# Convolution stages of layers 1 and 2: stores and residual loads on ScalarE's queue, image loads that wait for the products alone

## The chip, the cores and the metric

One core of a Trainium2 chip. The metric is the device time of one execution in microseconds (us).

## What is computed

An input x of 16 images of 32 channels of 128 x 128 float32 passes through four layers, each x = x + L(groupnorm(x)). Cut to what matters:

```python
# layer 1 begins with a convolution of the normalised image (18 offset channels, of which 9 are used)
offset = conv2d(gn(x), offset_conv_w, offset_conv_b, padding=[(1, 1), (1, 1)])   # 3 x 3
...
# layer 2 is one convolution, 32 to 32 channels, and the residual
x = x + (conv_general_dilated(gn(x), weight, (1, 1), ((1, 1), (1, 1))) + bias)   # 3 x 3
```

Layers 0 and 3 and the rest of layer 1 (a state-space model, a deformable gather) are untouched by the change.

## The kernel before, in words

The program runs one stage after the other, with a barrier of all engines between them. `conv_layer` (L508) is built twice: as stage `l1o` (layer 1, no residual, 16 channels stored, into `offsets`) and as stage `l2` (layer 2, with residual, 32 output channels, into the next x). Both handle B = 16 images, one after the other, with two buffers (u = 0, 1).

- **Load** (L536, SyncE): an image lands in `img` three times, shifted by one row up, none and one down, in partitions 0 to 31, 32 to 63 and 64 to 95 (dy = 0, 1, 2). Each copy is one DMA of 2032 or 2048 KB (L540), followed by a small one with the norm's scale and bias into `gn` (L542). With a residual, four DMAs of 512 KB follow (L546), which bring the same image again into `res`, a quarter of its rows in each quarter of the partitions.
- **Normalise** (L568, ScalarE): waits for the six DMAs of the image (`img_in`), and applies scale and bias in place in 11 activations (L575), then counts up `norm_done`.
- **Products** (L582, TensorE): for each of NS = 8 banks, 12 matmuls of 96 x 512 (L596), then `conv_done` goes up by one. The first bank of an image waits for `evac_done` of the image before.
- **Eviction** (L600, VectorE): waits for `stored[u]` and `res_in[u]`, then one instruction for each bank (L622 without a residual, L619 with one) adds bias (and residual) into `ot`, and `evac_done` goes up by one.
- **Store** (L549, SyncE): waits for the eight evictions of the image, then issues four DMAs (L553), of 256 KB each in `l1o` and of 512 KB in `l2`.

What orders the work around the change is SyncE's program: load(0), load(1), and then for each image i: store(i), with its wait, and behind it load(i + 2) into the buffer just used. An image load therefore stands behind the wait for the evictions, and behind the issue and the transfers of the store, in one queue. ScalarE issues no DMA in these stages.

Of the kernel before, what the change touches and what calls it, by code (L numbers as in the profile page):

```python
# [5 lines left out]
ACT = mybir.ActivationFunctionType  # L6
# [4 lines left out]
H = 128  # L11
W = 128
# [25 lines left out]
def at(first, n=1):  # L38

    return bass.ds(first, n)  # L40
# [467 lines left out]
def conv_layer(nc, stage, x, table, weights, bias, out, B, residual):  # L508
    C, WP = T, W + 2
    keep = out.shape[1]  # L510
    QR = H // 4
    RR = 512 // W
    NS = QR // RR
    with ExitStack() as ctx:
        m = Memory(nc, ctx, stage)
        img = m.sb("img", [P, 2, H, WP])
        gn = m.sb("gn", [3 * C, 2, 2])
# [11 lines left out]
        @block.sync  # L529
        def _(sp):  # L530
            sp.dma_start(wt[:, :, :], weights).then_inc(w_in, 16)
            for g in range(4):
                sp.dma_start(bc[C * g:C * (g + 1), :], bias.rearrange("(p a) -> p a", a=1)).then_inc(w_in, 16)
            sp.wait_ge(zeroed, 2)

            def load(b, u):  # L536
                for dy in range(3):
                    lo, hi = max(0, 1 - dy), min(H, H + 1 - dy)
                    part = slice(C * dy, C * (dy + 1))
                    sp.dma_start(img[part, u, lo:hi, 1:W + 1],  # L540
                                 x[at(b), :, lo + dy - 1:hi + dy - 1, :].rearrange("b c h w -> (b c) h w")).then_inc(img_in[u], 16)
                    sp.dma_start(gn[part, u, :], table.rearrange("b (c q) s -> b c q s", c=C)[at(b), :, 0, :].rearrange("b c s -> (b c) s")).then_inc(img_in[u], 16)  # L542

                if residual:
                    for q in range(4):
                        sp.dma_start(res[C * q:C * (q + 1), u, :],  # L546
                                     x[at(b), :, QR * q:QR * (q + 1), :].rearrange("b c h w -> (b c) (h w)")).then_inc(res_in[u], 16)

            def store(b, u):  # L549

                sp.wait_ge(evac_done, b * NS + 2 * NS)
                for q in range(4):
                    sp.dma_start(out[at(b), :, QR * q:QR * (q + 1), :].rearrange("b c h w -> (b c) (h w)"),  # L553
                                 ot[C * q:C * q + keep, u, :]).then_inc(stored[u], 16)

            load(0, 0)
            load(1, 1)
            with sp.Fori(0, B // 2 - 1) as j:
                for u in range(2):
                    store(j * 2 + u, u)  # L560
                    load(j * 2 + u + 2, u)
            for u in range(2):
                store(B - 2 + u, u)
            for u in range(2):
                sp.wait_ge(stored[u], (B // 2 + 1) * 64)

        @block.scalar
        def _(act):  # L568
            with act.Fori(0, B // 2) as j:
                for u in range(2):  # L570
                    act.wait_ge(img_in[u], j * 96 + 96)

                    def norm(part, rows):
                        v = img[part, u, rows, 1:W + 1]
                        return act.activation(v, v, ACT.Identity, scale=gn[part, u, 0:1], bias=gn[part, u, 1:2])  # L575

                    norm(slice(C, 2 * C), slice(0, 1))
                    norm(slice(2 * C, 3 * C), slice(0, 1))
                    norm(slice(0, 2 * C), slice(H - 1, H))
                    for k in range(NS):  # L580
                        ins = norm(slice(0, 3 * C), slice(max(1, k * H // NS), min(H - 1, (k + 1) * H // NS)))
                    ins.then_inc(norm_done, 1)  # L582

        @block.tensor
        def _(pe):
# [2016 lines left out]
```

## Time and profile before

| what | us |
|---|---|
| median of 3 runs | 24395.71 (24389.47 to 24419.06) |
| profiled execution, its own time | 24396.36 |
| its span in the trace | 24394.8 |
| stage `l1o`, from the barrier to the next stage | about 797 |
| stage `l2`, from the barrier to the next stage | about 883 |

The span is one execution as the hardware profiler records it, and the profiled execution's own time is 1.6 us above it. PE is TensorE, PEld its weight loads, DVE is VectorE, ACT is ScalarE, POOL is GpSimd; SPq and ACTq are DMA issues of SyncE and of ScalarE. Times of rows count from the start of the span. The share of the DMA engines can pass 1, since packets of one engine overlap.

### The profile page before, as it was taken

How to read it: one execution, taken by the hardware profiler on the slowest of the kernel's cores; microseconds unless marked ns; L12 is line 12 of the kernel's file. 1: busy time of each engine (PE TensorE's matmuls, PEld its weight loads, DVE VectorE, ACT ScalarE, POOL GpSimd, SP SyncE). 2: the span in 40 equal slices, each digit the busy share in tenths (PEclk: the TensorE clock that was granted, in tenths of full speed). 3: DMA queues.
4: the chain of work that ended last, by engine and by line, in shares of the span. 5: the costliest groups of instructions: out<-in, count | busy, mean ns of one | idle time of the engine just before them, and what ended most of it. 6: DMA issues, size and time to landing. Idle time of an engine off the chain costs nothing. (4 is left out here: it accounts for less than half of the span.)

```text
span 24394.8 us, 385684 instructions
## 1 busy us (share of the span) xinstructions
PE 19768.2 (81%) x135184; PEld 8014.9 (33%) x135184; DVE 15076.5 (62%) x15737; ACT 13799.3 (57%) x22826; POOL 8849.7 (36%) x5553
## 2 busy tenths in 40 slices
PE   6888888886438888888868999994468888888999
PEld 2333333332112222222215555551123333333444
DVE  8999999998138888888855666564143333333011
ACT  6889999896336666666636877783322222222111
POOL 6777778785017777777750000000000000000000
PEclk9999999998769999999988998797789999999999
DMA  1000000001950000000022111126920000111011
GB/s 65 11 12 12 11 12 12 12 11 64 158 116 18 18 18 18 18 17 18 18 69 35 34 34 37 30 38 151 198 71 23 23 23 23 29 24 30 31 43 43
DMA packets 1301498, 995.53 MB, mean 41 GB/s; under 512 B 748392, under 2 KB 1157584, under 8 KB 1265112
## 3 DMA queue, kind: packets, MB, share of 16 engines
q1 hardware_dynamic: 1199560, 849.64, 16.3%
q0 software_dynamic: 26624, 100.67, 1.5%
q10 hardware_dynamic: 74448, 33.14, 0.5%
q8 instruction: 608, 9.96, 0.2%
q14 instruction: 258, 2.11, 0.0%
HBM read 771.60 MB, written 211.63 MB: 40 GB/s over the span
## 5 line engine op out<-in xcount | busy, mean ns | idle before, releaser
L270 DVE TENSOR_TENSOR l_mx<-l_p_v,l_puN 128x2048 f32<-128x2048 f32 x2560 | 5636.5, 2282 | 151.6 <-PE l_p_s L485 138.7
L485 PE MATMUL l_p_s<-l_mx,l_w2z 128*32 128x512 f32 x32768 | 3827.9, 611 | 579.8 <-ACT l_mx L397 315.3
L290 POOL TENSOR_TENSOR l_mx<-l_pv,l_puP 128x2048 f32<-128x2048 f32 x1024 | 3715.6, 3644 | 321.8 <-PE l_p_s L485 316.0
L2103 PE MATMUL l3a_p<-l3a_xn,l3a_w 128*128 128x512 f32 (+1 forms) x6144 | 2680.9, 599 | 271.1 <-ACT l3a_xn L1994 271.1
L1157 DVE TENSOR_TENSOR_SCAN l1m_hs<-l1m_da,l1m_carry,l1m_pu 128x512 f32<-128x512 f32 x2304 | 2824.4, 1268 | 105.9 <-ACT l1m_da L1073 2.2
L2209 POOL DMA_DIRECT2D l3b_xt<-x_after x64 | 33.9, 529 | 7644.3 <-DVE l3b_most L2338 5818.0
L1206 POOL TENSOR_TENSOR l1m_hc<-l1m_hs,l1m_cs 128x1024 f32<-128x1024 f32 x1152 | 2708.7, 2351 | 9.2 <-DVE l1m_hs L1157 5.7
L1815 ACT ACTIVATE l1d_ab<-l1d_pt 128x1024 f32<-128x1024 f32 x2304 | 2299.4, 1024 | 706.9 <-PE l1d_pt L1569 693.0
L416 ACT ACTIVATE l_mx<-l_pv,l_puP 128x128 f32<-128x128 f32 x8192 | 2446.8, 393 | 0.8
L1693 DVE TENSOR_SCALAR l1d_hat<-l1d_ab 128x1024 f32<-128x1024 f32 x2304 | 1623.0, 704 | 818.9 <-ACT l1d_ab L1815 516.4
L397 ACT ACTIVATE l_mx<-l_mx 128x2048 f32<-128x2048 f32 x1024 | 1954.4, 1909 | 49.5 <-POOL l_mx L290 48.9
L485 PEld LDWEIGHTS l_p_s<-l_mx,l_w2z 128*32 128x32 f32 x32768 | 984.6, 112 | 3020.9 <-issue 1760.6
L1147 DVE TENSOR_TENSOR l1m_pu<-l1m_pu,l1m_bs 128x512 f32<-128x512 f32 x2304 | 1477.5, 687 | 749.3 <-PE l1m_pu L902 749.0
L1073 ACT ACTIVATE l1m_da<-l1m_pr,l1m_an 128x512 f32<-128x512 f32 x2304 | 1457.2, 683 | 823.4 <-PE l1m_pr L895 772.8
L902 PE MATMUL l1m_pu<-l1m_dts,l1m_sl 32*128 32x512 f32 x4608 | 1420.7, 692 | 534.8 <-ACT l1m_da L1073 525.9
L2231 PE MATMUL l3b_ps<-l3b_in,l3b_wc 128*128 (+2 forms) x3888 | 1638.2, 583 | 127.7 <-DMA l3b_in<-pooled 102.9
L2103 PEld LDWEIGHTS l3a_p<-l3a_xn,l3a_w 128*128 128x128 f32 (+1 forms) x6144 | 1094.1, 178 | 1857.9 <-issue 1857.9
L1604 PE MATMUL l1d_po<-l1d_hat,l1d_ring 128*32 128x128 f32 x36864 | 1640.6, 300 | 49.8 <-DVE l1d_hat L1693 45.8
L2118 PE MATMUL l3a_pc<-l3a_r,l3a_c 128*32 128x512 f32 x12288 | 1357.7, 605 | 270.7 <-issue 270.7
L1877 POOL TENSOR_TENSOR l1d_res<-l1d_res,l1d_xr 128x512 f32<-128x512 f32 x128 | 168.7, 1319 | 3540.6 <-ACT l1d_res L1824 3540.6
L895 PE MATMUL l1m_pr<-l1m_dts,l1m_sl 32*128 32x512 f32 x4608 | 1407.8, 689 | 2.7 <-ACT l1m_da L1073 2.7
L2005 ACT ACTIVATE l3a_r<-l3a_p 128x512 f32<-128x512 f32 x512 | 306.3, 598 | 1810.2 <-PE l3a_p L2103 1810.2
(301 smaller groups left out, 26624.6 us busy)
## 6 DMA issues: line engine op xcount, KB each, us to landing
n_xt<-x_after SPq DMA_DIRECT2D x48, 2048.0 KB
l3a_xb<-x_after SPq DMA_DIRECT2D x352, 256.0 KB, 4.1
l1o_img<-x_after SPq DMA_DIRECT2D x32, 2032.0 KB, 17.3
l_img<-x_after SPq DMA_DIRECT2D x32, 2032.0 KB, 16.9
l1m_sq<-seq SPq DMA_DIRECT2D x256, 144.0 KB
n_xt<-in_x_dram SPq DMA_DIRECT2D x16, 2048.0 KB
l_xs<-in_x_dram SPq DMA_DIRECT2D x128, 256.0 KB, 2.9
x_after<-l_ot SPq DMA_DIRECT2D x128, 256.0 KB, 2.4
```

Of the source, the lines that this page charges most:

```text
L270: v.tensor_tensor(mx[:, r % QB, :, :, :], columns.unsqueeze(1).broadcast_to([P, 4, G, P]), rows.broadcast_to([P, 4, G, P]), ALU.max).then_ ...
L290: g.tensor_tensor(mx[:, r % QB, :, :, :], pv[:, u, :, :].unsqueeze(1).broadcast_to([P, 4, G, P]), rows.broadcast_to([P, 4, G, P]), ALU.add ...
L397: act.activation(tile, tile, ACT.Relu).then_inc(max_by_g, 1)
L416: ins = act.activation(mx[:, r % QB, q, t, :], pv[:, u, t, :], ACT.Relu, bias=puP[:, u, t, R * q + r:R * q + r + 1])
L485: ins = pe.matmul(p_s[R * q:R * (q + 1), 512 * u:512 * (u + 1)], w2z[:, 31 - r:63 - r], mx[:, r % QB, q, :, :].rearrange("p t v -> p (t v) ...
L1157: dve.tensor_tensor_scan(hs[:, p % 3, part, :], da[:, p % 3, part, :], pu[:, LC * bank:LC * (bank + 1)], carry[:, u, c:c + 1], ALU.mult, A ...
L1206: g.tensor_tensor(hc[:, (3 * u + p) % 6], hs[:, p % 3], cs[:, u:u + 1, :].broadcast_to([NB, 2, LC]), ALU.mult).then_inc(hc_done, 2)
L1604: ins = pe.matmul(po[C * g:C * (g + 1), 512 * (s % 2):512 * (s % 2) + P], ring[:, (8 * u + s + k) % RING, g, k, :], hat[:, m % 3, n % 2, P ...
L1693: v.tensor_scalar(hat[:, m % 3], ab[:, m % 2], 1.0, 1.0, ALU.min, ALU.subtract).then_inc(hat_done, 1)
L1815: act.activation(ab[:, m % 2].rearrange("p a n -> p (a n)"), pt[:, 1024 * (m % 2):1024 * (m % 2 + 1)], ACT.Abs).then_inc(abs_done, 1)
L2103: ins = pe.matmul(acc[0:n, 512 * (ch % 2):512 * (ch % 2 + 1)], w[:, dx, :], xn[:, k % 2, r:r + RC, dx:dx + W], start=dx == 0, stop=dx == 2)
L2231: ins = pe.matmul(bank(name, u, rows * size), wc[:, k, tap, :], src[:, at((i + u) * rows + tap // 3, rows), tap % 3:tap % 3 + size], start ...
```

## The change

Stores and residual loads move from SyncE's program to ScalarE's, with four (`l1o`) or eight (`l2`) DMA issues for each image. ScalarE's order becomes: the residual loads of images 0 and 1, normalise(0), and then for each image i: normalise(i + 1), store(i) with its wait for the evictions, residual load(i + 2). SyncE keeps the image loads alone, and load(i + 2) waits for the 8 banks of image i in `conv_done` instead of `evac_done`. Sizes, matmuls, activations and evictions stay as they are.

```diff
--- before.py
+++ after.py
@@ -541,45 +541,56 @@
                                  x[at(b), :, lo + dy - 1:hi + dy - 1, :].rearrange("b c h w -> (b c) h w")).then_inc(img_in[u], 16)
                     sp.dma_start(gn[part, u, :], table.rearrange("b (c q) s -> b c q s", c=C)[at(b), :, 0, :].rearrange("b c s -> (b c) s")).then_inc(img_in[u], 16)
 
-                if residual:
-                    for q in range(4):
-                        sp.dma_start(res[C * q:C * (q + 1), u, :],
-                                     x[at(b), :, QR * q:QR * (q + 1), :].rearrange("b c h w -> (b c) (h w)")).then_inc(res_in[u], 16)
-
-            def store(b, u):
-
-                sp.wait_ge(evac_done, b * NS + 2 * NS)
-                for q in range(4):
-                    sp.dma_start(out[at(b), :, QR * q:QR * (q + 1), :].rearrange("b c h w -> (b c) (h w)"),
-                                 ot[C * q:C * q + keep, u, :]).then_inc(stored[u], 16)
-
             load(0, 0)
             load(1, 1)
             with sp.Fori(0, B // 2 - 1) as j:
                 for u in range(2):
+                    sp.wait_ge(conv_done, (j * 2 + u) * NS + NS)
+                    load(j * 2 + u + 2, u)
+
+        @block.scalar
+        def _(act):
+            def normalise(u, loads):
+                act.wait_ge(img_in[u], loads * 96)
+
+                def norm(part, rows):
+                    v = img[part, u, rows, 1:W + 1]
+                    return act.activation(v, v, ACT.Identity, scale=gn[part, u, 0:1], bias=gn[part, u, 1:2])
+
+                norm(slice(C, 2 * C), slice(0, 1))
+                norm(slice(2 * C, 3 * C), slice(0, 1))
+                norm(slice(0, 2 * C), slice(H - 1, H))
+                for k in range(NS):
+                    ins = norm(slice(0, 3 * C), slice(max(1, k * H // NS), min(H - 1, (k + 1) * H // NS)))
+                ins.then_inc(norm_done, 1)
+
+            def load_residual(b, u):
+                for q in range(4):
+                    act.dma_start(res[C * q:C * (q + 1), u, :],
+                                  x[at(b), :, QR * q:QR * (q + 1), :].rearrange("b c h w -> (b c) (h w)")).then_inc(res_in[u], 16)
+
+            def store(b, u):
+                act.wait_ge(evac_done, b * NS + 2 * NS)
+                for q in range(4):
+                    act.dma_start(out[at(b), :, QR * q:QR * (q + 1), :].rearrange("b c h w -> (b c) (h w)"),
+                                  ot[C * q:C * q + keep, u, :]).then_inc(stored[u], 16)
+
+            act.wait_ge(zeroed, 2)
+            if residual:
+                load_residual(0, 0)
+                load_residual(1, 1)
+            normalise(0, 1)
+            with act.Fori(0, B // 2 - 1) as j:
+                for u in range(2):
+                    normalise(1 - u, j + (1 + u))
                     store(j * 2 + u, u)
-                    load(j * 2 + u + 2, u)
+                    if residual:
+                        load_residual(j * 2 + u + 2, u)
+            normalise(1, B // 2)
             for u in range(2):
                 store(B - 2 + u, u)
             for u in range(2):
-                sp.wait_ge(stored[u], (B // 2 + 1) * 64)
-
-        @block.scalar
-        def _(act):
-            with act.Fori(0, B // 2) as j:
-                for u in range(2):
-                    act.wait_ge(img_in[u], j * 96 + 96)
-
-                    def norm(part, rows):
-                        v = img[part, u, rows, 1:W + 1]
-                        return act.activation(v, v, ACT.Identity, scale=gn[part, u, 0:1], bias=gn[part, u, 1:2])
-
-                    norm(slice(C, 2 * C), slice(0, 1))
-                    norm(slice(2 * C, 3 * C), slice(0, 1))
-                    norm(slice(0, 2 * C), slice(H - 1, H))
-                    for k in range(NS):
-                        ins = norm(slice(0, 3 * C), slice(max(1, k * H // NS), min(H - 1, (k + 1) * H // NS)))
-                    ins.then_inc(norm_done, 1)
+                act.wait_ge(stored[u], (B // 2 + 1) * 64)
 
         @block.tensor
         def _(pe):
```

## Rows read from the trace of the kernel before

**Rows 1.** Both stages (windows): busy us of five engines, TensorE clock, DMA share, GB/s
```profile
6079.00:6876.00 797.00, 365.65 (x3072) 97.88 (x3072) 124.12 (x135) 274.23 (x176) 0.00 (x0) 0.73 0.98 147
16790.00:17673.00 883.00, 364.46 (x3072) 97.58 (x3072) 124.10 (x135) 274.25 (x176) 0.00 (x0) 0.71 1.03 190
```

**Rows 2.** Who waited for whom, layer 1's stage, then layer 2's
```profile
ACT l1o_img L575 <- DMA l1o_gn<-norm_table: 498.8, 16, 82.9
...
SPq L553 <- DVE l1o_ot L622: 74.8, 12, 38.6
...
SPq L553 <- DVE l_ot L619: 45.1, 2, 44.7
```

**Rows 3.** Timeline of layer 1's stage, one image: start us, us, engine and line
```profile
6328.38 17.17 ACT L575 ACTIVATE l1o_img<-l1o_img,l1o_gn 32x128 f32<-32x128 f32 x11 [28.77 <-DMA l1o_gn<-norm_table]
...
6355.47 11.47 SPq L542 DMA_DIRECT2D l1o_gn<-norm_table  x1
...
6368.61 0.75 DVE L622 TENSOR_SCALAR l1o_ot<-l1o_acc,l1o_bc 128x512 f32<-128x512 f32 x1 [1.82 <-PE l1o_acc L596]
6369.53 5.18 SPq L553 DMA_DIRECT2D offsets<-l1o_ot  x4
...
6374.90 1.99 SPq L540 DMA_DIRECT2D l1o_img<-x_after  x1
```

**Rows 4.** Timeline of layer 2's stage, SyncE's queue, one image
```profile
17054.31 1.87 SPq L546 DMA_DIRECT2D l_res<-x_after  x4
17056.47 1.85 SPq L553 DMA_DIRECT2D x_after<-l_ot  x4
```

**Rows 5.** Timeline: first load of layer 2's stage, and ScalarE's normalisations
```profile
16824.83 0.32 SPq L540 DMA_DIRECT2D l_img<-x_after  x1
...
16863.67 17.16 ACT L575 ACTIVATE l_img<-l_img,l_gn 32x128 f32<-32x128 f32 x11 [83.02 <-DMA l_gn<-norm_table]
16910.05 17.17 ACT L575 ACTIVATE l_img<-l_img,l_gn 32x128 f32<-32x128 f32 x11 [29.21 <-DMA l_gn<-norm_table]
16961.64 17.17 ACT L575 ACTIVATE l_img<-l_img,l_gn 32x128 f32<-32x128 f32 x11 [34.42 <-DMA l_gn<-norm_table]
...
17619.73 17.17 ACT L575 ACTIVATE l_img<-l_img,l_gn 32x128 f32<-32x128 f32 x11 [33.49 <-DMA l_gn<-norm_table]
...
6238.52 17.17 ACT L575 ACTIVATE l1o_img<-l1o_img,l1o_gn 32x128 f32<-32x128 f32 x11 [36.76 <-DMA l1o_gn<-norm_table]
...
6822.33 17.17 ACT L575 ACTIVATE l1o_img<-l1o_img,l1o_gn 32x128 f32<-32x128 f32 x11 [26.08 <-DMA l1o_gn<-norm_table]
```

**Rows 6.** Transfer rate within single phases of an image (windows; last column GB/s)
```profile
16957.00:16966.00 9.00, 0.00 (x0) 0.00 (x0) 0.00 (x0) 4.33 (x5) 0.00 (x0) 0.50 1.09 221
16967.00:16970.00 3.00, 0.00 (x0) 0.00 (x0) 0.00 (x0) 3.00 (x3) 0.00 (x0) 0.50 0.93 360
16974.00:16981.00 7.00, 2.06 (x12) 0.61 (x16) 0.00 (x0) 4.80 (x3) 0.00 (x0) 0.50 1.25 174
16986.00:16993.00 7.00, 7.00 (x68) 1.93 (x64) 2.25 (x3) 0.00 (x0) 0.00 (x0) 1.00 1.02 177
6281.00:6287.00 6.00, 0.00 (x0) 0.00 (x0) 0.00 (x0) 4.53 (x5) 0.00 (x0) 0.55 1.21 142
```

**Rows 7.** DMA packets of an image's first copy, then of its second
```profile
DMA packets 2375, 1.21 MB, mean 174 GB/s; under 512 B 2, under 2 KB 2375, under 8 KB 2375
...
DMA packets 128, 1.05 MB, mean 175 GB/s; under 512 B 0, under 2 KB 0, under 8 KB 0
```

**Rows 8.** Two queues at once, in 12625 to 12630 us: packets, MB, share
```profile
q1 hardware_dynamic: 418, 0.83, 67.7%
q10 hardware_dynamic: 411, 0.11, 12.3%
```

**Rows 9.** Timeline at 12620 us: DMA issues of ScalarE and of SyncE
```profile
12620.08 11.97 ACTq L1325 DMA_DIRECT2D rows<-l1y_piece  x1
...
12630.03 0.30 SPq L1275 DMA_DIRECT2D l1y_f<-seq  x1
```

## The prediction

> **What bounds the kernel now.** First the busy times of the two stages: in 797 and 883 us the fullest compute engine, TensorE, works 366 us, while the DMA share is 0.98 and 1.03 [rows 1]. So the transfers are full and no engine is. The table of waits says the same: in `l1o` ScalarE's idle time, 498.8 us, all ends with the image's DMAs [rows 2]. What the change can touch is how SyncE keeps the queue filled. In `l2` its wait for the evictions cost 45.1 us in only 2 waits, 44.7 of them the last one, after all loads: over the 14 images between it never waits, so the queue never runs out. In `l1o` there are 12 waits, 74.8 us; without the last (38.6 us) that is 36.2 us in 11, some 3.3 us each [rows 2]. In the timeline the reader sees how close it is: the eviction ends at 6369.36, four store issues take 5.18 us, and only at 6374.90 the next image load goes out [rows 3].
>
> Then the sizes. An image is 2.10 MB; it is copied three times (6.26 MB, two copies lack a row), the residual is 2.10 MB, the store 2.10 MB in `l2` and 1.05 MB in `l1o`. Rates by phase [rows 6]: image copies 174 to 177 GB/s, residual 221, store of `l2` 360, store of `l1o` 142. That makes 35.8 us for the copies, 9.5 for the residual, 5.8 and 7.4 us for the stores. Sum for `l2`: 51.1 us an image; ScalarE's normalisations start 13 x 50.6 us apart from the third to the last (16961.64 to 17619.73) [rows 5]. **`l2` is its transfers, one after the other.** Sum for `l1o`: 43.2 us; measured 44.9 (6238.52 to 6822.33 over 13) [rows 5]. The 1.7 us are the queue running dry around the waits.
>
> A second bound is the turn of one buffer, which carries every second image. From the start of a normalisation to the end of the last eviction: 6328.38 to 6369.36, 41.0 us [rows 3]; from the issue of a load on an empty queue to its normalisation: 16824.83 to 16863.67, 38.8 us [rows 5].
>
> **The change, part by part.**
>
> *The wait and the issue ahead of the image load.* The load waits for `conv_done`, one eviction (0.75 us) earlier than before, and the 5.2 us of store issue are gone from SyncE (in `l2` 1.87 + 1.85 us for eight issues [rows 4]). Behind SyncE's new wait stand image loads alone. In `l1o` a buffer's turn becomes 40.2 + 38.8 us plus the store's 7.4 us of transfer, which still falls into every load: 86.4, or 43.2 us an image, by chance the same as the sum of the transfers (40.2 is 41.0 less the 0.75). So of the 1.7 us at most all goes. Two bounds that meet seldom both hold without a gap, and the store now stands at another place of the load, so I take half, 0.8 us: 13 x 0.8 = 10 us less. Ends: 0 and 22 us less. In `l2` a turn is (40.2 + 38.8 + 15.3)/2 = 47.2 us an image, under 50.6; the transfers bound it, and the earlier release is worth nothing, because what covers it is the image load still under way.
>
> *Eight (four) issues on ScalarE.* ScalarE works 17.2 us for an image [rows 5] and has 33.4 us to spare in `l2`, 27.7 in `l1o`. At SyncE's price the issues cost it 3.7 and 5.2 us, beside the transfers: nothing. Store(i) now goes out behind normalise(i + 1), when evictions of i have long ended (41.0 us after normalise(i) began, with the next normalisation ending at 50.6 + 17.2), so its wait is free; its store is needed, and the residual too, only at the first eviction of i + 2, some 50 us later. Nothing is late there.
>
> *Two queues on the same DMA engines.* No stage of the change has shown this, so I bound it by the one place where both queues are full, at 12625 us: SyncE's queue 418 packets of 2 KB, ScalarE's 411 of 256 bytes [rows 8]. The engines take one packet from each in turn, whatever its size. An image's first and third copies are packets of 512 bytes (1.21 MB in 2375), its second of 8 KB (1.05 MB in 128) [rows 7]; stores and residuals I take to be as large or larger. So when ScalarE's burst comes, the image stream all but stands, for the 15.3 us (7.4 in `l1o`) that the burst would have taken in line anyway: **the sum stays**. Only against the second copy's packets would there be real sharing, and the burst begins 17.2 us and a few us of latency after an image has landed, when the second copy (11.9 to 23.9 us) is nearly through. I take a gain of 0.5 us an image in `l2`, 13 x 0.5 = 6.5 us less; ends: 2 us of gain (26 us less) to 0.5 us of loss from disturbing (6.5 more). The Trainium skill, "DMA: Bandwidth & Descriptors", section "Queues, rings and completion order", says that an engine drains a whole packet, typically 9 to 17 descriptors, from one queue before it turns to the next. If the 512-byte pieces went in such groups, the image stream would go on during the burst, which is the second rival's case; the equal counts above speak for single pieces.
>
> *Residual loads at the start and end of `l2`.* Before, residual 0 followed image 0, residual 1 image 1, and residual 15 came last, hidden under the last normalisation. Now residuals 0 and 1 go out with image 0: normalise(0) comes 2 x 9.5 = 19 us later, at 16882.7, image 1 lands 9.5 us later than its 16910.05, at 16919.6, and the products of image 0 end at 16882.7 + 40.2 = 16922.9, with the queue dry for some 5 us. Image 2 is normalised at 16922.9 + 38.8 + 15.3 = 16977, against 16961.64: **15 us more**, never won back, since transfers bound the rest. Ends: 10 (the residual's own time alone) and 20. `l1o` has no residual.
>
> Sum: -10 - 6.5 + 15 = -1.5 us, on the profiled execution's 24396.36 us (span 24394.8): 24395. The runs' median, 24395.71, is the same to 0.7 us. With the ends: from -22 - 26 + 10 = -38 to 0 + 6.5 + 20 = +27, 24358 to 24423.
>
> **The rivals.**
>
> *Faster: the burst is hidden in the image stream.* For it: image copies move only 175 GB/s, stores 360 [rows 6], so an engine that waits on a small copy could move a store meanwhile. Against it: the one-for-one turn. If half of each burst were hidden, `l2` would take max(35.8 + 7.65, (79.0 + 7.65)/2) = 43.5 us an image: 13 x 7.1 less, 15 more, 77 us less; `l1o` max(39.5, 41.4) = 41.4: 13 x 3.5 = 46 less. Together 24273.
>
> *Slower: ScalarE's issues wait behind SyncE's.* The small DMA behind an image copy sits in issue for 11.47 us [rows 3], while that copy's packets are made. If making them held up ScalarE's issues too, its normalisations would start late, in `l2`, where it issues eight. It decides from 33.4/8 = 4.2 us an issue. At one long wait for every two issues, 4 x 11.5 + 17.2 = 63.2 us an image: 13 x 12.6 = 164, and 15: 24575 (in `l1o`, 2 x 11.5 + 5.2 + 17.2 = 45.4, no change worth counting). Against it: ScalarE's issue of 11.97 us from 12620.08 was under way when SyncE issued at 12630.03 in 0.30 us [rows 9]. The Trainium skill, "Perfetto Trace Analysis", section "DMA Instruction — HWDGE (DVE, Sync)", has descriptor generation as one block, locked for one sequencer at a time; by that rule this rival would hold, and the row says that it is no lock for the length of an issue.
>
> **How the numbers follow.** About 0.2% (49 us) is what a measurement of this kernel can tell from no change. My forecast gets 0.78: its ends lie within 0.2%, but terms that I have not seen may carry 0.03 of it below and 0.01 above. Hidden bursts get 0.16, of which 0.01 would stay within 0.2%; held-up issues 0.06. So faster 0.03 + 0.15 = 0.18, same 0.74 + 0.01 = 0.75, slower 0.01 + 0.06 = 0.07. The range takes my ends, widened below to 24335 for bursts hidden in a small part, above to 24428; about 2 in 10 lie outside, in the rivals' full prices.
>
> **What would show it.** In the changed kernel: normalisations of `l2` 50 us apart from the third on, those of `l1o` 44; the first of `l2` some 58 us after the first load's issue instead of 38.8; SyncE's image loads waiting for TensorE, not for VectorE; ScalarE's issues of 0.3 to 1.3 us each. `l1o` some 787 us, `l2` some 892. I am wrong if the interval in `l2` is under 48 us (bursts hidden), or if ScalarE shows issues of several us (held up), or if the DMA rate during a burst is well above the two phases' own.

## The result, and the profile after

| what | before | after |
|---|---|---|
| median of 12 runs each, side by side | 24401.65 (24341.51 to 24473.11) | 24321.45 (24244.69 to 24380.95) |
| ratio to before, with its 95% interval | 1 | 0.9962 (0.9948 to 0.9976) |
| profiled execution, its own time | 24396.36 | 24289.5 |
| its span | 24394.8 | 24287.9 |

The changed kernel is 80 us faster by the medians, and by the interval 59 to 127 us faster. The forecast was 24395, with 24335 to 24428 around it: it said no change, and the time came out below the range.

Where did it go? First the two stages, in windows from stage start to stage end (columns as in [rows 1]).

```profile
6074.00:6799.00 725.00, 367.82 (x3072) 98.71 (x3072) 123.98 (x133) 274.25 (x176) 0.00 (x0) 0.74 0.96 161
16686.00:17565.00 879.00, 366.98 (x3072) 98.79 (x3072) 123.58 (x133) 274.24 (x176) 0.00 (x0) 0.71 1.02 190
```

TensorE, VectorE and ScalarE do what they did before, in 725 us instead of 797 in `l1o`, in 879 instead of 883 in `l2`. The rate in `l1o` rose from 147 to 161 GB/s [rows 1]. Measured in the same way for every kernel below, from the first instruction of one stage to that of the next:

| stage | before | after | difference |
|---|---|---|---|
| `l1o` | 799.6 | 730.0 | -69.6 |
| `l2` | 882.7 | 884.0 | +1.3 |
| deformable gather, untouched | 3827.5 | 3783.9 | -43.6 |
| all others | 18885.0 | 18890.0 | +5 |

The two stages of the change give -68 us, which lies inside the interval. The 43.6 us of the gather are its own scatter: over the profiled executions of this case it took 3764 to 3910 us with the same instructions. So the experiments are read by the lengths of the two stages, which repeat within 2 us in `l1o` (730.0, 731.3 and 731.3 in the changed kernel, e8 and e9, whose `l1o` loops are the same). In `l2` they repeat less well: in four kernels whose `l2` loop is the same (the changed kernel, e9, e10 and e11) the distance between two normalisations was 49.5, 48.8, 47.9 and 49.5 us, a spread of 1.6 us an image or 21 us a stage.

The normalisations (start us, us, engine, line) give the distance: in `l1o` from the third to the last 13 x 40.2 us, where it was 44.9 [rows 5]. In `l2` the first comes 58.0 us after the first load's issue (first row of the second fence), the third 152.4, and from there it is 13 x 49.5 to the last, where it was 50.6 [rows 5].

```profile
6225.68 0.99 ACT L558 ACTIVATE l1o_img<-l1o_img,l1o_gn 32x128 f32<-32x128 f32 x2 [28.87 <-DMA l1o_gn<-norm_table]
6748.57 1.00 ACT L558 ACTIVATE l1o_img<-l1o_img,l1o_gn 32x128 f32<-32x128 f32 x2 [23.34 <-DMA l1o_gn<-norm_table]
```

```profile
16716.88 0.33 SPq L540 DMA_DIRECT2D l_img<-x_after  x1
...
16774.85 0.99 ACT L558 ACTIVATE l_img<-l_img,l_gn 32x128 f32<-32x128 f32 x2 [102.70 <-DMA l_gn<-norm_table]
...
16869.24 0.99 ACT L558 ACTIVATE l_img<-l_img,l_gn 32x128 f32<-32x128 f32 x2 [42.03 <-DMA l_gn<-norm_table]
...
17513.20 0.99 ACT L558 ACTIVATE l_img<-l_img,l_gn 32x128 f32<-32x128 f32 x2 [31.45 <-DMA l_gn<-norm_table]
```

Now the waits of SyncE in the changed `l1o` (engine and line waiting, what it waited for: total us, times, longest), and of ScalarE in the same stage:

```profile
SPq L540 <- PE l1o_acc L607: 84.4, 14, 10.6
ACT l1o_img L558 <- DMA l1o_gn<-norm_table: 429.5, 16, 82.4
```

The image load waits for TensorE, 14 times, 6 us each. Before, SyncE waited in front of the stores, 3.3 us in 11 waits [rows 2]. A wait that is longer in a stage that is shorter means that SyncE had sent off the last image load early: in `l1o` the queue is no longer what is short, the turn of one buffer is. In `l2` there is one such wait, for image 2 at the start, where the prediction had the queue run dry for some 5 us; over the rest the transfers bound it still:

```profile
SPq L540 <- PE l_acc L607: 11.6, 1, 11.6
```

The timeline around one store of `l1o` shows where the store went (start us, us, engine, line):

```profile
6385.11 8.40 SPq L542 DMA_DIRECT2D l1o_gn<-norm_table  x1
6386.29 1.50 ACT L558 ACTIVATE l1o_img<-l1o_img,l1o_gn 32x128 f32<-32x128 f32 x3 [25.24 <-DMA l1o_gn<-norm_table]
6387.55 0.32 ACTq L575 DMA_DIRECT2D offsets<-l1o_ot  x1
6387.70 1.97 ACT L558 ACTIVATE l1o_img<-l1o_img,l1o_gn 96x1920 f32<-96x1920 f32 x1
6388.03 1.27 ACTq L575 DMA_DIRECT2D offsets<-l1o_ot  x3
```

ScalarE issues the four DMAs in 1.8 us here (5.18 us on SyncE before [rows 3]; in 6 of the loop's 14 images they took ScalarE 4.9 to 5.1 us as well), and not behind its normalisation but 1.3 us after that has begun, while its activations run. What the engines then move, in windows of GB/s (last column) of the image copy before the store's packets, of a store with few image packets beside it, and of a store beside image packets:

```profile
6388.00:6393.00 5.00, 0.00 (x0) 0.00 (x0) 0.00 (x0) 5.00 (x3) 0.00 (x0) 0.50 1.26 174
6394.00:6398.00 4.00, 0.00 (x0) 0.00 (x0) 0.00 (x0) 4.00 (x3) 0.00 (x0) 0.50 1.14 319
6353.00:6360.00 7.00, 0.00 (x0) 0.00 (x0) 0.00 (x0) 7.00 (x5) 0.00 (x0) 0.50 1.12 284
```

The image copy runs at its old 174 GB/s [rows 6]; store and copy together come to 319 and 284. The store's own 1.05 MB in the second window passed in 3.6 us, 290 GB/s, where before it took 9.6 us (109 GB/s) from its first packet to its last. The packets of that third window by queue (q1 is SyncE's, q10 ScalarE's: packets, MB, share):

```profile
q1 hardware_dynamic: 1896, 0.97, 68.7%
q10 hardware_dynamic: 124, 1.02, 43.0%
```

In 7 us nearly the whole store (1.02 of 1.05 MB) and 0.97 MB of image came through; the image alone would have moved 1.22 MB at 174 GB/s. The store cost the image 1.4 us here, not 7.4, and the queues did not take turns one for one. Of ScalarE's 124 packets 62 are the store's, of 16 KB; the other 62 have 4 bytes. So 62 packets of the store stand against some 1890 of the image.

In `l2` a burst is a store and a residual load. Its window, 17 us from 17024, shows less of this: 0.86 MB of image beside 3.93 MB, where the image alone would have moved 2.96 MB.

```profile
q10 hardware_dynamic: 347, 3.93, 80.7%
q1 hardware_dynamic: 1058, 0.86, 29.0%
```

The two halves of the burst differ. The first two lines are 7 us of the store (17024 to 17031), the next two 9 us of the residual load (17032 to 17041):

```profile
q10 hardware_dynamic: 165, 1.88, 67.4%
q1 hardware_dynamic: 878, 0.55, 46.1%
...
q10 hardware_dynamic: 149, 1.69, 89.6%
q1 hardware_dynamic: 145, 0.28, 17.8%
```

Beside the store 878 packets of the image queue went by with 165; beside the residual load 145 with 149, and the image got 0.28 MB in 9 us, where alone it would have moved 1.57. (Some of ScalarE's packets have 4 bytes; 115 and 103 have 16 KB.) Store and residual load have the same packets of 16 KB on the same queue. **The store lets the image stream by; the residual load takes turns with it, nearly one for one**, as the prediction had it for both. At the head of the stage, where the residual loads of images 0 and 1 meet the first image copy, the image stands as well: in 18 us 0.21 MB of it in 416 packets passed, beside 3.64 MB, 222 packets of 16 KB.

```profile
q10 hardware_dynamic: 325, 3.64, 94.7%
q1 hardware_dynamic: 416, 0.21, 7.4%
```

### The profile page after: what moved, and what is told of

The parts are those of the page before. It is cut to its first block and busy times, and to the rows that moved or that the text cites. A ratio compares the mean times of both kernels' runs of the same rounds, so it can differ in the third digit from the quotient of the medians.

```text
span 24287.9 us, 385739 instructions
## 1 busy us (share of the span) xinstructions
PE 19733.4 (81%) x135184; PEld 7979.7 (33%) x135184; DVE 15078.0 (62%) x15737; ACT 13796.1 (57%) x22826; POOL 8850.6 (36%) x5553
## 5 line engine op out<-in xcount | busy, mean ns | idle before, releaser
L1615 PE MATMUL l1d_po<-l1d_hat,l1d_ring 128*32 128x128 f32 x36864 | 1610.0, 295 | 53.1 <-DVE l1d_hat L1704 48.9
```

Source lines behind the costliest of these rows:

```text
L1615: ins = pe.matmul(po[C * g:C * (g + 1), 512 * (s % 2):512 * (s % 2) + P], ring[:, (8 * u + s + k) % RING, g, k, :], hat[:, m % 3, n % 2, P ...
```

## The experiments

Theory 1 at the outset was that `l1o` gained because the image load no longer stands behind the store, whichever queue the store is on; theory 2, that it gained because a burst on a second queue hides in the image stream. The normalisations' distance below is from the third to the last, over 13. All stage lengths are in us. e1 to e6 and e9 to e11 ran once each, e8 six times, e7 four times:

| kernel | `l1o` | distance | `l2` | distance |
|---|---|---|---|---|
| before | 799.6 | 44.9 | 882.7 | 50.6 |
| after | 730.0 | 40.2 | 884.0 | 49.5 |
| e1 one queue | 764.2 | 42.9 | 885.2 | 51.4 |
| e2 load waits for evictions | 737.0 | 40.7 | 876.7 | 48.9 |
| e3 store behind the normalisation | 728.0 | 40.1 | 882.0 | 49.6 |
| e4 third copy on ScalarE's queue | 717.1 | 39.4 | 787.5 | 44.5 |
| e5 no bursts in the loop | (822.5) | 39.1 | (857.3) | 39.1 |
| e6 second copy on ScalarE's queue | 684.2 | 37.0 | 775.0 | 43.2 |
| e7 third copy there, small packets | 675.2 | 36.8 | 751.9 | 42.1 |
| e8 residuals behind normalise(0) | 731.3 | 40.3 | 854.2 | 47.9 |

**e1_one_queue.** Everything back on SyncE, in the new order:

```diff
-                    store(j * 2 + u, u)
-                    load(j * 2 + u + 2, u)
+                    sp.wait_ge(conv_done, (j * 2 + u) * NS + NS)
+                    load(j * 2 + u + 2, u)
+                    store(j * 2 + u, u)
+                    if residual:
+                        load_residual(j * 2 + u + 2, u)
```

> Everything stays on SyncE's queue; only the order changes: the image load goes out first, behind the wait for the products, and the store (and the residual load) behind it. If the gain of the change is the order (the image load no longer stands behind the store), layer 1's convolution stage takes 730 to 745 us, as in the changed kernel (730), and not 800 as before. If the gain needs a second queue, whose packets take turns with the image's, the stage stays at 785 to 800 us. Layer 2's stage: 880 to 890 us by either.

Measured: 24315.14 us (24411.69 before on the same chip); `l1o` 764.2, which is 35.4 us of the 69.6. The store is as slow as it was, four issues in 5.17 us (first row), and the distance is 42.9 us, the sum of the transfers of the prediction (43.2) to 0.3 us. SyncE waits for the products once only, for image 2 at the start (second row: a wait of SyncE), so in the loop its queue never ran dry: on one queue, the sum does bound `l1o`.

```profile
6377.21 5.17 SPq L553 DMA_DIRECT2D offsets<-l1o_ot  x4
```

```profile
SPq L540 <- PE l1o_acc L603: 10.2, 1, 10.2
```

The stage lies between the two ranges of the expectation. So about half of the gain is the order (the queue stays full), and the other half, 34 us, needs the second queue. Both theories hold a half. The half of theory 1 was in my sum, as an end: I had taken 10 us where its full 22 us and an earlier third image (9.4 us here) were to be had.

**e2_evac_wait.** The changed kernel, whose image load waits for the evictions again:

```diff
-                    sp.wait_ge(conv_done, (j * 2 + u) * NS + NS)
+                    sp.wait_ge(evac_done, (j * 2 + u) * NS + 2 * NS)
```

> The changed kernel with the image load waiting for the evictions instead of the products. If a buffer's turn bounds layer 1's stage, each turn is 0.75 us longer and the stage 5 to 8 us longer, 735 to 738 us; if the transfers bound it, no change (730). Layer 2's stage unchanged, 884 us.

Measured: 24284.94 us; `l1o` 737.0, 7 us more than the changed kernel, 0.5 us an image. An image load that is held up by an eviction of 0.75 us, and pays it, is bound by the buffer's turn. `l2` shows no cost: 876.7, within what its loop scatters by.

**e3_late_store.** ScalarE waits for the end of its own normalisation ahead of the store, as the prediction had assumed it would:

```diff
                     normalise(1 - u, j + (1 + u))
+                    act.wait_ge(norm_done, j * 2 + u + 2)
                     store(j * 2 + u, u)
```

> The changed kernel with ScalarE waiting for the end of each normalisation before it issues the store, as my prediction took it to be (17 us later than it was). If the early place of the burst made the gain, layer 1's stage goes back towards my 787 us (43 to 44 us an image) and layer 2's to 890 and more. If a store costs little wherever it meets a running image copy, the stages stay at 730 and 884 us within 8 us.

Measured: 24242.67 us; 728.0 and 882.0. The wrong place of the burst in the prediction was worth next to nothing: 2 us in either stage, the other way.

**e4_third_copy.** The third copy of the image (dy = 2, into partitions 64 to 95) goes out on ScalarE's queue, between store and residual load:

```diff
-                for dy in range(3):
+                for dy in range(2):
...
                     store(j * 2 + u, u)
+                    load_third(j * 2 + u + 2, u)
```

> The changed kernel with the third copy of each image (partitions 64 to 95) issued on ScalarE's queue, ahead of the residual. If two queues' packets really flow side by side and a copy of 32 partitions does not fill the engines, the first image is normalised 25 to 30 us after the first load instead of 38, and layer 1's stage falls to 620 to 680 us, layer 2's below 800. If the descriptors of both queues are made one DMA after the other, copies follow each other as before: 38 us, and stages of 725 to 745 and 880 to 895 us.

Measured: 24290.99 us as a whole, with a gather of 3909.8 us in it; the stages are 12.9 and 96.5 us shorter than the changed kernel's. `l2` fell below 800 as expected; `l1o` missed its 620 to 680 us, and its first normalisation came 36.8 us after the first load, not 25 to 30. Two copies of 512-byte packets side by side moved 289 and 294 GB/s (one stretch of each stage), where one alone moves 174 [rows 6]:

```profile
6096.00:6106.00 10.00, 0.00 (x0) 0.00 (x0) 0.00 (x0) 0.00 (x0) 0.00 (x0) 0.50 1.20 289
17036.00:17045.00 9.00, 5.12 (x28) 1.31 (x32) 0.00 (x0) 3.75 (x2) 0.00 (x0) 0.53 1.20 294
```

Beside the second copy, whose packets have 8 KB, the third copy stood almost still. In the 10 us from 6108 (SyncE's queue, then ScalarE's; both move 185 GB/s together):

```profile
q1 hardware_dynamic: 213, 1.74, 94.2%
q10 hardware_dynamic: 213, 0.11, 7.8%
```

Here the turns are one for one, whatever the size, as in the prediction: 213 packets of 8 KB and 213 of 512 bytes.

It also showed that the rival "ScalarE's issues wait" is real for such copies, though not for stores:

```profile
6103.90 24.85 ACTq L571 DMA_DIRECT2D l1o_gn<-norm_table  x1
6128.79 7.35 ACT L558 ACTIVATE l1o_img<-l1o_img,l1o_gn 32x128 f32<-32x128 f32 x6 [80.88 <-issue]
```

The small DMA behind the copy held ScalarE for 24.85 us, and the first normalisation, which stands behind it, began when that ended ("<-issue").

**e5_no_burst.** No store and no residual load in the loops, and evictions that do not wait for them:

```diff
                     normalise(1 - u, j + (1 + u))
-                    store(j * 2 + u, u)
-                    if residual:
-                        load_residual(j * 2 + u + 2, u)
```

> The changed kernel with the stores and residual loads left out of the loops of both convolution stages (all 16 stores follow at the stage's end, from buffers that hold other images; the residual of images 2 to 15 is that of images 0 and 1), to see what the bursts cost each image. A buffer's turn alone gives (40.2 + 38.8)/2 = 39.5 us between normalisations. If that is what bounds layer 1's stage now, its interval falls from 40.2 only to 39.5; if the store still took its 7.4 us of transfers as I had it, to 36 to 37 us. Layer 2's interval falls from 49.5 to the same 39.5, so the burst of store and residual costs it 10 us there.

Measured: 24396.6 us. Only the distance counts here. It is 39.1 us in both stages (rows of the third and the last normalisation, first of `l1o`, then of `l2`), where the prediction's two pieces of a turn give (40.2 + 38.8)/2 = 39.5. **The bare turn of a buffer is 39.1 to 39.5 us an image.** In the changed `l1o` it is 40.2; a turn takes two images, so the store adds 2 x (40.2 - 39.1) = 2.2 us to a turn, not 7.4.

```profile
6208.61 0.99 ACT L558 ACTIVATE l1o_img<-l1o_img,l1o_gn 32x128 f32<-32x128 f32 x2 [26.24 <-DMA l1o_gn<-norm_table]
...
6716.28 1.00 ACT L558 ACTIVATE l1o_img<-l1o_img,l1o_gn 32x128 f32<-32x128 f32 x2 [20.20 <-DMA l1o_gn<-norm_table]
...
16990.67 0.99 ACT L558 ACTIVATE l_img<-l_img,l_gn 32x128 f32<-32x128 f32 x2 [25.54 <-DMA l_gn<-norm_table]
...
17499.18 0.99 ACT L558 ACTIVATE l_img<-l_img,l_gn 32x128 f32<-32x128 f32 x2 [20.28 <-DMA l_gn<-norm_table]
```

The 16 stores at the end ran on ScalarE's queue with nothing beside them, one behind the other, at 143 GB/s, half of the 290 of the changed kernel's store at 6394. A single store alone takes 9.6 us on SyncE's queue (before) and on ScalarE's (the changed kernel's last two). It is not the queue that makes a store slow:

```profile
6790.00:6870.00 80.00, 0.00 (x0) 0.00 (x0) 0.00 (x0) 0.00 (x0) 0.00 (x0) 0.50 0.93 143
```

**e6_same_partitions and e7_even_packets.** One copy goes to ScalarE's queue, and the second (dy = 1) is cut into 127 rows and one, so that it too moves in packets of 512 bytes. In e6 it is that copy (partitions 32 to 63) that ScalarE loads, in e7 the third (64 to 95); e7 issues the residuals of images 0 and 1 behind normalise(0), too. From e7:

```diff
-                for dy in range(3):
-                    lo, hi = max(0, 1 - dy), min(H, H + 1 - dy)
...
+                copy(sp, b, u, 0, ((1, H),))
+                copy(sp, b, u, 1, ((0, H - 1), (H - 1, H)))
...
+            def load_other(b, u):
+                copy(act, b, u, 2, ((0, H - 1),))
...
                     store(j * 2 + u, u)
+                    load_other(j * 2 + u + 2, u)
```

> The changed kernel with the second copy (partitions 32 to 63) on ScalarE's queue, its last row in a DMA of its own so that its packets are 512 bytes too, beside the first copy (partitions 0 to 31) on SyncE's. The third copy beside the first (the run before) moved 290 GB/s against 174 for one alone. If a second queue is what frees the engines, this pair moves 290 GB/s too. If the limit is in where in the 128 partitions the data lands, some pairs of groups do not gain: this one stays at 175 to 200 GB/s for both together.

> First and second copy on SyncE's queue, third on ScalarE's, all in packets of 512 bytes, and the residual loads of images 0 and 1 behind normalise(0). If one-for-one turns held the third copy back beside the second's 8 KB packets, layer 2's interval falls under the 45 us of the run before, to 41 to 43, and layer 1's to 36 to 38; the whole kernel is 130 to 200 us faster than the kernel before. If ScalarE, held while its own queue is full, is what bounds now, the intervals stay at 39 and 45 us, and the kernel is 100 to 130 us faster.

Measured: e6 24178.41 us; e7 24079.62, ratio 0.9881 (0.9859 to 0.9902). e6's trace holds both cases in its first 36 us. From 6096 to 6112 the copies into partitions 0 to 31 and 32 to 63 run side by side, from 6120 to 6128 those into 32 to 63 and 64 to 95. The windows and then the packets of the two queues in each:

```profile
6096.00:6112.00 16.00, 0.00 (x0) 0.00 (x0) 0.00 (x0) 0.00 (x0) 0.00 (x0) 0.50 1.26 172
6120.00:6128.00 8.00, 0.00 (x0) 0.00 (x0) 0.00 (x0) 0.00 (x0) 0.00 (x0) 0.50 1.20 290
```

```profile
q10 hardware_dynamic: 2683, 1.37, 63.5%
q1 hardware_dynamic: 2684, 1.37, 62.7%
...
q1 hardware_dynamic: 2264, 1.16, 60.4%
q10 hardware_dynamic: 2270, 1.16, 59.7%
```

The queues take turns packet by packet in both, 2684 to 2683 and 2264 to 2270. Side by side below partition 64, two copies share what one has, 172 GB/s; on either side of it they get 290. The packets and the queues are the same in both; the partitions differ. So does the source: the first pair reads one image, the second two. But the pair of e4 reads one image too, into partitions 0 to 31 and 64 to 95, and moved 289 GB/s, so it is the partitions. e7, whose pairs lie on either side from the start, keeps this up:

```profile
6092.00:6112.00 20.00, 0.00 (x0) 0.00 (x0) 0.00 (x0) 0.00 (x0) 0.00 (x0) 0.50 1.20 289
```

The Trainium skill, "SBUF — State Buffer", section "Door 1: The DMA port swizzle (why `[64,N]` ≈ `[32,N]`)", says that a DMA reaches 8 of 16 ports with partitions 0 to 31, the same 8 with 0 to 63, and the other 8 with 64 to 127. The trace agrees: 172 GB/s for a pair below 64, 290 for a pair across. The same page's section '"Can I just issue two DMAs to hit both halves?"' says that such a pair gains only 6% over one copy. That differs here: 290 against 174 is 67% more for packets of 512 bytes on two queues, and the measurement decides.

e6's stages are 9.0 and 23.1 us longer than e7's. Of e7's gain in `l2` a part is the order at the start (next run), so the pairing alone is worth less than these 23 us. In `l1o`, which has no residual, the pairing is 9.0 of the 54.8 us by which e7 is under the changed kernel. There e7 differs from e4 by the packets of the second copy alone, and is 41.9 us shorter (717.1 to 675.2, distance 39.4 to 36.8). So most of the gain in `l1o` is the second copy's small packets: in e4 the third copy stands beside packets of 8 KB. As a whole e7 beats both kernels: with its interval 0.9881 of before, where the change has 0.9962. Both distances came out in the ranges of the first case expected; the whole is 297 us faster by the medians, more than the 130 to 200, of which the two stages give 255.

**e8_head.** The changed kernel, with the first residual loads behind the first normalisation:

```diff
+            normalise(0, 1)
             if residual:
                 load_residual(0, 0)
                 load_residual(1, 1)
-            normalise(0, 1)
```

> The changed kernel with the residual loads of images 0 and 1 issued behind normalise(0) instead of ahead of it. The first normalisation of layer 2's stage comes 39 us after the first load instead of 58, and the stage is 5 to 10 us shorter (874 to 879 us), since the queue no longer runs dry before image 2; if the dry stretch is not what made the stage longer, it stays at 884. Layer 1's stage unchanged.

Measured: 24261.41 us, ratio 0.9959 (0.9946 to 0.9973); `l2` 854.2, 29.8 less than the changed kernel, more than I had expected. Of these, 9.1 are the start: the third normalisation comes 143.3 us after the first load's issue, against 152.4. The other 21 are a shorter distance, 47.9 instead of 49.5 us, 13 times; but that is the spread between kernels with the same loop (e10 has 47.9 too), so they are not shown to come from the edit. The start is shown by the stage: in the changed kernel, e9, e10 and e11 the third normalisation comes after 151.1 to 153.2 us. The whole kernel's interval can't tell 30 us from the changed kernel's.

**e9_primed, e10_long_prime, e11_company.** What makes a store of `l1o` take 9.6 us in one place and 3.6 to 7.7 in another? Three runs changed only the last two stores of each stage. e9 puts a small load (31 rows, 992 packets of 512 bytes) ahead of each on ScalarE's queue, e10 a whole copy (256 packets of 8 KB), and e11 puts a copy of 4064 packets of 512 bytes on SyncE's queue beside each:

```diff
             for u in range(2):
+                act.wait_ge(evac_done, (B + u) * NS)
+                act.dma_start(img[0:C, u, 1:H // 4, 1:W + 1],
+                              x[at(B - 2 + u), :, 0:H // 4 - 1, :].rearrange("b c h w -> (b c) h w")).then_inc(primed, 16)
                 store(B - 2 + u, u)
```

> The changed kernel with a small extra load (31 rows of 32 channels, 992 packets of 512 bytes, into a part of the image buffer that nothing reads any more) on ScalarE's queue ahead of each of the last two stores of both stages. Without it these two stores meet an idle queue, and in l1o they take 9.6 us each, 2180 ns a packet of 16 KB, issue 5.1 us for the four. Theory A (the wait makes it fast): a store whose descriptors all lie written behind other packets runs at full speed; then behind the extra load the 64 packets of the last stores take some 600 to 800 ns each and the store 4 us, on the very same queue. Theory B (company on the other queue makes it fast): on a lone queue a store of 16 partitions at a time takes 2180 ns a packet whatever lies ahead; then it stays at 9.6 us from its first packet to its last. Theory C (the issue sets the pace): four issues of 1.3 us or more each while the packets move, and 0.3 to 0.4 us each where the packets do not move yet. The time of the whole is that of the changed kernel within 20 us, since two extra loads of some 4 us stand in each stage's tail.

> As the run before, but the extra load ahead of each of the last two stores is a whole unshifted copy of an image (256 packets of 8 KB, about 12 us at the 174 GB/s of such copies), on ScalarE's queue. The small extra load of the run before lasted 2 to 3 us, and the store behind it still took 8.6 and 8.7 us at some 1730 to 1800 ns a packet. Theory A (standing written for several us makes it fast, on any queue): the four issues take 0.3 to 0.4 us each while the extra load's packets move, and the store's 64 packets then run at 600 to 800 ns, some 4 us. Theory B (a store is fast only when its packets are let in between those of another queue): it still takes 8 to 10 us and 1700 to 2200 ns a packet. The whole: that of the changed kernel and some 15 us in each stage's tail.

> The changed kernel with an extra load on SyncE's queue (127 rows of 32 channels, 4064 packets of 512 bytes, 12 us alone, into a part of the image buffer that nothing reads any more), released by the same count of evictions as each of the last two stores of both stages, which go out on ScalarE's queue in the same moment. Theory A (standing written makes it fast): the store's packets start at once, 2 us after the issue, as they did alone, and so take 1700 ns or more each, since nothing made them wait; at one for one with the small packets the store ends in about 9 us. Theory B (company makes it fast): 600 to 900 ns a packet though they start at once. If the packets stand back for 6 us or more, as they do in the stage's body, SyncE's copy itself is what holds them, and they then run at 600 to 900 ns. The whole: that of the changed kernel and 10 to 20 us.

Measured, in `l1o`: e9 8.6 and 8.7 us for the two stores, with 1726 and 1806 ns a packet (24270.9 us); e10 6.7 and 6.3 us, 1283 and 1265 ns (24367.68 us); e11 10.3 us for both, but only 901 and 904 ns a packet (24309.83 us). In e10 ScalarE was held in issue behind the copy's packets:

```profile
6737.59 7.94 ACTq L576 DMA_DIRECT2D offsets<-l1o_ot  x1
6745.55 2.47 ACTq L576 DMA_DIRECT2D offsets<-l1o_ot  x2
6748.05 2.74 ACTq L576 DMA_DIRECT2D offsets<-l1o_ot  x1
```

The copy ended at 6750.7. The 31 packets of the store that started first, up to 6751.4, took 0.6 to 1.3 us each; of the other 33, 27 took 1.4 to 2.5 us. In e9 the first 16 took 0.7 to 1.5 us, the next 16 1.7 to 2.7. In e11 16 packets started beside the copy 2.4 us after the first issue and took 0.8 to 2.2 us, 1.36 us in the mean; the other 48 began only 3 us after these had ended, behind SyncE's packets, and took 0.6 to 0.9 us. For the most part all three speak for theory A, packet by packet: what stands ready and has had to wait is fast. The 16 of e11 took less than the 2.2 us of a lone store, which A does not cover. But the result that counts for the change is e11's window, copy and store together:

```profile
6738.00:6752.00 14.00, 0.00 (x0) 0.00 (x0) 0.00 (x0) 14.00 (x8) 0.00 (x0) 0.51 1.05 221
```

A copy of 12 us alone (2.08 MB at 174 GB/s) and a store of 9.6 us alone took 14 us together. **Beside small image packets the store is hidden but for some 2 us**, and that is the 2.2 us that e5 gives from another side. Why a packet that has stood ready takes 611 ns rather than 2180 stays open.

A lone store's own 9.6 us have a plain reading: four DMAs of 256 KB in 2.4 us each are 109 GB/s from the first packet to the last (the window of [rows 6] counts in full each packet that starts in its 6 us, hence its 142), and each reads 16 partitions. The Trainium skill, "SBUF — State Buffer", in the same section on Door 1, has 104 GB/s measured for partitions 0 to 15, with a limit near 109, and the trace agrees. By that rule four such DMAs at once could not pass 218 GB/s, an estimate, though; the 290 GB/s of the store above differ from it, and no run here explains them.

## Why the prediction was wrong, point by point

- **What bounds the kernel.** Right: the transfers, not an engine, and for `l2` their sum: 51.1 predicted, 50.6 measured before, 51.4 on one queue in e1. For `l1o` the sum of 43.2 was right as well (42.9 in e1), and the turn's two pieces are right to 0.4 us (e5). Its 7.4 us for a store are not the time of a lone one, which is 9.6 us; in the kernel before, the next copy's packets started 1.8 us ahead of the store's end, and the image's packets stood still for 5 to 7 us.
- **The step that failed is "the sum stays"**: that the engines take one packet from each queue in turn, whatever its size, so that an image stream all but stands while a burst passes. For two streams of loads that is right or nearly so: 2264 to 2270 with 512 bytes in both (e6), 213 to 213 with 8 KB beside 512 bytes (e4), and 149 to 145 with a residual load's 16 KB beside the image in `l2`. It is wrong for a store. In its window in `l1o` some 1890 packets of the image went by with 62 of the store, in `l2` 878 with 165. The rule came from [rows 8], two queues at one place; I took it over to the stores, for which no row stood. What lets the image by a store and not by a load of the same packets no run shows. From it followed the second error, a term of the sum: the store's 7.4 us in a buffer's turn. It measured 2.2 (e5), so the distance fell to 40.2 us, where one queue has 42.9 (e1): 13 x 2.7 = 35 us, the half of the gain that needs the second queue.
- **The other term of `l1o`**, the queue that ran dry, was mis-sized: I took half of 1.7 us an image, 10 us. e1 shows that all of it goes, 13 x 2.0 = 26 us, and the first images come 9.4 us sooner besides, which I had not counted. Two bounds that meet cost nothing here, since in the loop the queue does not wait for the turn even once (e1: one wait of SyncE, at the start). The 35.4 us of e1 and the 34.2 of the second queue are the 69.6.
- **The earlier release** counts where the turn bounds: 7 us in `l1o` (e2), nothing that can be told in `l2`. The prediction gave it its 0.75 us in the turn, but let the transfers' sum hide it.
- **Eight issues on ScalarE: no cost.** Right. They cost it less than SyncE, in `l1o` 0.32 us by the median of 64 (0.99 on SyncE before), and run beside its activations. Their place, in most images 1.3 us after a normalisation's start and not 17.2, was wrong and harmless (e3).
- **The head of `l2`, +15.** Right: the first normalisation comes 58.0 us after the first load (16716.9 to 16774.85; predicted 58), the third 152.4 (predicted 152.2). e8 takes 9.1 of it back.
- **`l2` in its steady state** gained 1.1 us an image, 14 us, where I took 6.5; it is inside the ends I gave. So head and gain cancel, +1.3, where I had +8.5. But the other kernels with the same loop gained 1.1 to 2.7 us, so this stage's figure is one draw, and the upper end of my gain (2) is passed by some. The gain stays small because of the residual load, for which the rule of turns holds.
- **The rivals.** "The burst is hidden" was the one that came true, in `l1o` alone: where its 46 us for half of the burst hidden stand against 69.6; its 7.1 us an image in `l2` were 1.1, since there only the store is hidden. The profile before held the hint, an image stream at 174 GB/s beside a store at 360, and I gave it 0.16 because of one row on turns. "ScalarE's issues wait behind SyncE's" did not happen with stores and residuals, whose issues return at once; their packets did wait, 5.1 to 7.5 us from the issue to the store's first packet in the loop of `l1o`, where a lone store has 0.8. With the image's copies it did, up to 24.85 us (e4), but behind its own queue's packets.
- **The rule of the Trainium skill** on queues ("DMA: Bandwidth & Descriptors", section "Queues, rings and completion order"), that an engine drains 9 to 17 descriptors from one queue before it turns, was set against the equal counts. The trace has equal counts for streams of loads, and some 1890 to 62 beside a store; it fits neither the rule nor my reading of it in both places. Equal counts alone do not speak for single pieces, as I wrote, since equal groups give them too; e4 does: in each of the 10 us from 6108, 19 to 23 packets of either queue started on the 16 engines, some 1.3 an engine. What it would have made of the time, the image going on during the burst, came true in `l1o`.

## What to carry to other kernels

Before a DMA queue is called full, look at its GB/s by phase, and at which partitions each phase touches: 174 GB/s beside phases of 360 is a stream with room beside it, and on a second queue a store, or a copy in packets of the same size to the other side of partition 64, fits into it. A load in larger packets does not: it takes turns one for one and holds the stream up. A rule about how two queues share, read from two loads, should not be carried to a store without giving the opposite case a good share of the chance. And when transfers and a buffer's turn nearly meet, work out both without the other's waits: the order of loads and stores alone gave half of this gain on one queue, and its cost or gain is in the distance between two uses of a buffer.

## What the runs showed of the hardware

- Two copies of 512-byte packets into partitions 0 to 31 and 32 to 63 share 172 GB/s; into partitions on either side of 64 they reach 290 (e6, e7). In e7 that shortens the first image's load in `l2` from 38.8 us [rows 5] to 31.0:

```profile
16685.05 0.32 SPq L532 DMA_DIRECT2D l_img<-x_after  x1
...
16716.02 1.00 ACT L561 ACTIVATE l_img<-l_img,l_gn 32x128 f32<-32x128 f32 x2 [75.20 <-DMA l_gn<-norm_table]
```

- Two queues of loads take turns packet by packet, small ones beside large ones too: 2264 to 2270 (512 bytes each, e6), 213 to 213 (8 KB and 512 bytes, e4). So 8 KB packets on one queue leave 0.11 MB in 10 us to 512-byte packets on the other. A store beside a load does not keep to this: 62 packets to some 1890 in `l1o`.
- A store of 64 packets of 16 KB, 16 partitions a DMA, takes 9.6 us alone on either queue (109 GB/s). When it has stood behind SyncE's packets for 5 to 7.5 us, its packets take 705 to 798 ns each in the mean (2180 alone), and the store 3.6 to 4.9 us in 8 of the loop's 14 images and 7.0 to 7.7 us in the other 6, with 0.9 to 1.2 MB of image going by meanwhile. Its issue costs about 1.3 us a DMA alone and in those 6 images, and 0.4 to 0.9 in the others.
- ScalarE's DMA issues run ahead of its own activations: 1.3 us after the first of eleven, the store's first issue is out, unless a wait on `norm_done` holds it (e3).
- The small DMA that follows an image copy is held in issue while that copy's packets move: 7.5 to 11.8 us on SyncE's queue in the changed `l1o`, behind copies of 256 packets (9.77 us from 6358.15) as behind those of 4064, and 27.12 us at the head of `l2`, where residual loads pass. On ScalarE's queue it was 24.85 us and held up the next normalisation (e4).
